# Weight dequantisation moved out of the projection stage onto GpSimd in the attention stage, its loads issued twice a slot by SyncE

## What is computed

```
x = x + attention(layernorm(x))      # 32 heads of width 16, causal, biases on q, k, v, o
x = x + ffn(layernorm(x))            # gate/up 512x1792, down 1792x512, 4-bit weights held as int32
x = x + topk_mlp(layernorm(x))       # 1376 wide, the half with the smallest |silu| set to zero
x = x + ffn(layernorm(x))            # the same quantised weights again
```

## Time and profile before

| what | us |
|---|---|
| median of 3 runs (2161.17, 2175.11, 5822.98) | 2175.11 |
| the profiled execution, its own time | 2164.9 |
| its span, first to last instruction | 2163.1 |
| stage 1 (start to the last matmul) | 184.4 |
| stage 2 (187.7 to the end of slot 15) | about 583 |
| mean granted TensorE clock | 0.969 |

### The profile page before, as it was taken

The page is one execution under the profiler, slowest core; times in us unless marked ns, Lnnn a source line. Parts: engine busy times, 40 slices in busy tenths (PEclk is TensorE's granted clock), DMA queues, the critical chain, the costliest instruction groups (busy, mean ns, idle before and its releaser), DMA issues. The chain is left out here.

```text
span 2163.1 us, 38405 instructions
## 1 busy us (share of the span) xinstructions
PE 2014.5 (93%) x14288; PEld 1236.3 (57%) x14288; DVE 1565.1 (72%) x2736; ACT 1020.2 (47%) x1658; POOL 560.5 (26%) x587
## 2 busy tenths in 40 slices
PE   5887999999999977899999999999999999999989
PEld 2342344444444344677667667666666666666756
DVE  6775677777777432169888988978889889788941
ACT  3221356565655621156366454553664545535511
POOL 2223453842523332111210311212103112121221
PEclk9997799999999988999999999999999999999999
DMA  7766235432333164020222013013130130131000
GB/s 258 234 214 176 70 95 137 126 86 68 93 95 83 33 196 167 9 98 1 87 72 100 6 53 120 6 53 119 59 125 1 54 115 1 53 115 53 11 11 11
DMA packets 115656, 187.35 MB, mean 87 GB/s; under 512 B 43200, under 2 KB 68176, under 8 KB 115520
## 3 DMA queue, kind: packets, MB, share of 16 engines
q1 hardware_dynamic: 91344, 133.22, 19.9%
q0 software_dynamic: 9088, 32.12, 5.3%
q10 hardware_dynamic: 15088, 20.19, 2.7%
HBM read 151.59 MB, written 33.62 MB: 86 GB/s over the span
## 5 line engine op out<-in xcount | busy, mean ns | idle before, releaser
L842 DVE TENSOR_REDUCE mx<-s 128x1 f32<-128x512 f32 (+3 forms) x608 | 380.9, 660 | 128.8 <-PE s L731 75.0
L823 ACT ACTIVATE pr<-s 128x1024 f32<-128x1024 f32 (+3 forms) x352 | 300.7, 868 | 243.8 <-PE s L750 181.7
L1467 ACT ACTIVATE kept<-ax,T 128x1376 f16<-128x1376 f32 x248 | 357.0, 1439 | 122.0 <-DVE T L1541 116.1
L1535 DVE TENSOR_SCALAR_CACHE_REDUCE junk<-ax,T 128x1376 f16<-128x1376 f32 x248 | 406.5, 1639 | 3.1 <-DVE T L1528 0.5
L1326 POOL TENSOR_TENSOR lohi<-h,lohi 128x256 f16<-128x256 f32 x224 | 173.6, 775 | 872.9 <-ACT lohi L1478 872.7
L1364 PE MATMUL ga<-xT_f,w_gate 128*128 128x256 f16 x2688 | 332.7, 274 | 7.9 <-DVE h L1592 4.9
L1374 PE MATMUL acc<-w_down,lohi 128*128 128x512 f16 x1344 | 326.3, 379 | 8.7 <-POOL lohi L1326 8.7
L1364 PE MATMUL ub<-xT_f,w_up 128*128 128x256 f16 x2688 | 331.6, 273 | 0.0
L1364 PEld LDWEIGHTS ga<-xT_f,w_gate 128*128 128x128 f16 x2688 | 263.3, 98 | 79.9 <-DVE h L1592 7.5
L1364 PEld LDWEIGHTS ub<-xT_f,w_up 128*128 128x128 f16 x2688 | 263.9, 98 | 31.2
L728 PE MATMUL s<-K,Q 65*128 65x512 f16 (+3 forms) x768 | 245.2, 345 | 26.3 <-DMA K<-onerow 13.5
(11 more groups left out here) (142 smaller groups left out, 2352.5 us busy)
## 6 DMA issues: line engine op xcount, KB each, us to landing
ring<-wgu_scr SPq DMA_DIRECT2D x64, 688.0 KB, 5.3
ring<-wd_scr SPq DMA_DIRECT2D x24, 768.0 KB, 4.7
wgu_scr<-tk_h POOLq DMA_DIRECT2D x16, 344.0 KB, 6.0
q_scr<-qk_h ACTq DMA_DIRECT2D x16, 256.0 KB, 4.0
k_scr<-qk_h ACTq DMA_DIRECT2D x16, 256.0 KB, 2.5
v_scr<-v_f ACTq DMA_DIRECT2D x16, 256.0 KB, 2.9
Q<-q_scr SPq DMA_DIRECT2D x32, 128.0 KB
K<-k_scr SPq DMA_DIRECT2D x32, 128.0 KB
```

The lines of the kernel that those rows point to most:

```text
L823: nc.scalar.activation(pr[:, kb % 2, j0:j1, 0:w], scores, ACT.Exp, scale=SCALE).then_inc(e2_ok, 1)
L842: nc.vector.tensor_reduce(dst, s1[u % 2][:, 0:(j1 - j0) * w].rearrange("p (j k) -> p j k", k=w), AX.X, ALU.max).then_inc(r1_ok, 1)
L1467: nc.scalar.activation(kept[0][:, :], ax[k % 2][:, 1, :], ACT.Sign, scale=-1.0, bias=TF[:, 1:2], accum_out=cnt[:, 1:2]).then_inc(c1_ok, 1)
L1535: nc.vector.tensor_scalar(junk[:, :], ax[k % 2][:, 0, :], TF[:, 0:1], -float(KZERO), ALU.is_lt, ALU.add, accum_out=cnt[:, 0:1]).then_inc(c ...
```

## The change

`phase_project` loses the 16 pieces on all five engines. With them gone it is rewritten in these points: ACT writes `qk_f` and the float16 `qk_h` from PSUM, two activations in a row, and DVE's cast is gone; the stores move from ACT to SP and have four buffers instead of two; the transposes have four PSUM banks instead of two; the raw weights have three buffers instead of two; the q weights are loaded and split in four parts, the first two tiles are normalised before the others, and k and v weights are split in slots 0 and 1.

`phase_attend` gets all quantised weights: 32 pieces 128x448 of gate and up and 14 pieces 128x512 of down, each five POOL operations. The third block's weights come in 32 pieces 128x344 and 11 of 512 columns, each with three POOL operations and one store instead of two. POOL's work is spread over 32 half slots. SP issues all loads, in two packs a slot, one between half 0 of Q and K and the maxima row, one between V and the output's store; each load waits for the buffer of three (or four) pieces before. V beside ones of slot n + 1 is done at the middle of slot n in POOL's program. SP's loop is written out.

```diff
             for s in range(SLOTS):
                 c, u = s // SPC, s % SPC
                 if u < QK_SLOTS:
...
-                    nc.scalar.activation(qk_f[:, u % 2, :], pmm[u % 4][:, :], ACT.Identity,
-                                         bias=bias_qk[:, u // KB, u % KB:u % KB + 1], scale=QS / (XS * WS)
-                                         ).then_inc(qkf_ok, 1)
+                    nc.scalar.activation(qk_f[:, u % 2, :], pmm[u % 4][:, :], ACT.Identity, bias=bias,
+                                         scale=QS / (XS * WS))
+                    wait(act, qk_st[u % NST], 16 * (v // NST))
+                    nc.scalar.activation(qk_h[:, u % NST, 0, :], pmm[u % 4][:, :], ACT.Identity, bias=bias,
+                                         scale=QS / (XS * WS)).then_inc(qkf_ok, 1)
+                if s < 2:
+                    weight_hi(s + 1)
...
-                    nc.vector.tensor_copy(qk_h[:, u % 2, 0, :], qk_f[:, u % 2, :]).then_inc(qkh_ok, 1)
-                    dve.wait_ge(qkh_ok, v + 1)
...
+        NDQ = len(dq_pieces)
+        UNITS = 2 * NQ
+        dq_unit = [m * UNITS // NDQ for m in range(NDQ)]
+        dq_load = [dq_unit[m - NDB] + 1 if m >= NDB else 0 for m in range(NDQ)]
...
+        tk_unit = [m * UNITS // NTK for m in range(NTK)]
+        tk_load = [tk_unit[m - NRAW] + 1 if m >= NRAW else 0 for m in range(NTK)]
...
+            def load_pieces(unit):
+                for m in range(NDQ):
+                    if dq_load[m] == unit:
+                        width, wsrc, zsrc, ssrc, _dst = dq_pieces[m]
+                        wait(sp, dq_lo, m - NDB + 1)
+                        for dst, src in ((dq_w, wsrc), (dq_z, zsrc), (dq_s, ssrc)):
+                            sp.dma_start(dst[:, m % NDB, 0:width], src).then_inc(dq_in[m % NDB], 16)
...
+            for n in range(NQ):
+                if n + 2 < NQ:
+                    load_qk(n + 2, 0)
+                load_pieces(2 * n + 1)
+                if n + 1 < NQ:
+                    maxima_row(n + 1)
+                if n + 2 < NQ:
+                    load_qk(n + 2, 1)
+                    load_v(n + 2)
+                load_pieces(2 * n + 2)
+                store(n)
...
+            def dequantise(m):
+                width, _w, _z, _s, (hi, lo) = dq_pieces[m]
+                value, raw, zero, scale = (t[:, m % NDB, 0:width] for t in (dq_f, dq_w, dq_z, dq_s))
+                pool.wait_ge(dq_in[m % NDB], 48 * (m // NDB + 1))
+                nc.gpsimd.tensor_tensor(raw, raw, zero, ALU.subtract).then_inc(dq_sub, 1)
+                pool.wait_ge(dq_sub, m + 1)
+                nc.gpsimd.tensor_scalar(value, raw, WS, 1.0, ALU.mult, ALU.mult).then_inc(dq_up, 1)
+                pool.wait_ge(dq_up, m + 1)
+                nc.gpsimd.tensor_tensor(value, value, scale, ALU.mult).then_inc(dq_mul, 1)
+                pool.wait_ge(dq_mul, m + 1)
+                nc.gpsimd.tensor_copy(hi, value).then_inc(dq_hi, 1)
+                pool.wait_ge(dq_hi, m + 1)
+                nc.gpsimd.tensor_tensor(lo, value, hi, ALU.subtract).then_inc(dq_lo, 1)
+
+            beside_ones(0)
+            for unit in range(UNITS):
+                if unit % 2 and unit // 2 + 1 < NQ:
+                    beside_ones(unit // 2 + 1)
+                for m in range(NDQ):
+                    if dq_unit[m] == unit:
+                        dequantise(m)
+                for m in range(NTK):
+                    if tk_unit[m] == unit:
+                        split_weights(m)
```

More of the change, by code:

```diff
@@ L116, in phase_project @@
     QK_SLOTS = 2 * KB
+    NTR = 4
+    NST = 4
     with ExitStack() as ctx:
@@ L184, in phase_project @@
-        NPIECE = len(pieces)
+        qk_st = [sem(f"qk_st{i}") for i in range(NST)]
+        v_st = [sem(f"v_st{i}") for i in range(NST)]
         SLOTS = NCH * SPC
-        slot_of = [2 + n * (SLOTS - 5) // NPIECE for n in range(NPIECE)]
-        piece_at = {s: n for n, s in enumerate(slot_of)}
-        assert len(piece_at) == NPIECE and slot_of[-1] + 2 < SLOTS
         RSTD_AT, XN_AT = 2, 4
         block = ctx.enter_context(nc.Block())
[L194 to L198, removed]
@@ L200, in _, with load_x @@
         @block.sync
         def _(sp):
[L202 to L208, removed]
+            def load_x(c):
+                wait(sp, xn_ok, TPC * (c - 1))
+                sp.dma_start(xin[:, c % 2, :, :], x[c * CW:(c + 1) * CW, :].rearrange("(t p) d -> p t d", p=P)
+                             ).then_inc(x_in[c % 2], 16)
@@ new lines, in _ @@
+            for s in range(SLOTS):
+                c, u = s // SPC, s % SPC
+                if u < QK_SLOTS:
+                    n = QK_SLOTS * c + u
+                    sp.wait_ge(qkl_ok, n + 1)
+                    sp.dma_start((q_scr, k_scr)[u // KB][(u % KB) * P:(u % KB + 1) * P, :, c * CW:(c + 1) * CW],
+                                 qk_h[:, u % NST, :, :]).then_inc(qk_st[u % NST], 16)
+                else:
+                    n = TPC * c + u - QK_SLOTS
+                    sp.wait_ge(vf_ok, n + 1)
+                    sp.dma_start(v_scr[n * P:(n + 1) * P, :], v_f[:, n % NST, :]).then_inc(v_st[n % NST], 16)
+                if s == 3:
+                    load_x(2)
+                if s == SPC + 2:
+                    load_x(3)
@@ L224, in _ @@
+            for i in range(NST):
+                sp.wait_ge(qk_st[i], 16 * QK_SLOTS // NST * NCH)
+                sp.wait_ge(v_st[i], 16 * TPC // NST * NCH)
         @block.gpsimd
@@ L529, in phase_attend @@
         o_out = [sem(f"o_out{i}") for i in range(2)]
-        tk_in = [sem(f"tk_in{i}") for i in range(2)]
+        tk_in = [sem(f"tk_in{i}") for i in range(NRAW)]
         tk_up = sem("tk_up")
@@ new lines, in load_pieces @@
+            def load_pieces(unit):
[6 more added lines that the diff above has]
+                for m in range(NTK):
+                    if tk_load[m] == unit:
+                        rows, width, src, _dst = tk_pieces[m]
+                        wait(sp, tk_lo, m - NRAW + 1)
+                        sp.dma_start(tk_raw[0:rows, m % NRAW, 0:width], src).then_inc(tk_in[m % NRAW], 16)
@@ new lines, in _ @@
+            for n in range(2):
+                for f in range(2):
+                    load_qk(n, f)
+                load_v(n)
+            load_pieces(0)
+            maxima_row(0)
+            for n in range(NQ):
[9 more added lines that the diff above has]
+                store(n)
```

363 lines of the change are left out of this document (134 added, 229 removed).

## The result

| | us |
|---|---|
| before, median on the chip of this comparison | 2171.14 |
| after, median | 2156.12 |
| ratio, with 95% interval | 0.9947 (0.9929 to 0.9965) |
| profiled execution of after, span | 2154.3 (before 2163.1) |

The time lies in the forecast's range and the sign is right, but of 24 us forecast 11 to 15 came. Behind that stand two errors of opposite sign, which partly cancel: stage 1 gained 36.0 us, not 30, and stage 2 lost 26, not 6.

The account below looks back on a forecast made before the run. PE bounds stage 2; in stage 1 PE waits for `xn` from DVE. Stage 1 was to lose 30 us (32.5 - 5.5 + 3.4) and stage 2 to add 6: 2164.9 - 30 + 6 = 2141 us, range 2126 to 2176.

Parts of the forecast that it names:

- Term 1: Stage 1: PE's waits for `xn` and the slow restarts after them go, 32.5 us less.
- Term 2: Stage 1: new short waits of PE's transposes for `xn`, 0.4 us for each of 12 groups, 5.5 us more in all.
- Term 3: Start of stage 1: PE's first product comes 3.4 us earlier, at 14.9 us.
- Term 4: Stage 2: POOL's added work fits, 25 us of a 33.3 us slot, price 0.
- Term 5: Stage 2: the maxima row queues behind the pack's loads, 0 to 1.3 us late in 8 slots, 5 us more.
- Term 6: Stage 2: DVE's small maximum ahead of the row is slowed by a running POOL operation; price 0, bound 7 us.
- Term 7: Stage 2: POOL's stores of split weights, 43 instead of 38, collide once more with a row, 1 us more.
- The slower rival: Stage 2: maxima row late in every slot behind transfers issued ahead, 42 us over 15 slots; 2177, up to 2189 us; 12%.
- Its second price: Stage 2, row late in every slot: 15 slots cost 54 us if the pack moves at 246 GB/s instead of 280.

Follow-up runs that it names:

- experiment 4: The changed kernel, but SP issues both packs of weight loads behind V, none ahead of the maxima row: 2130.28 us, ratio 0.9813.
- experiment 7: The changed kernel with POOL's scalings written with one operation, without the second multiplication by 1: ratio 0.995.
- experiment 2: The changed kernel, but SP waits for the maxima row to land before issuing half 1 of Q and K: 2147 us, ratio 0.9899.
- experiment 6: Kernels with both packs behind V, plus chosen amounts of data ahead of the maxima row in five slots: 2145.9, 2142.3, 2149.0 and 2138.6 us.
- the first experiment: The changed kernel with SP's odd pack of loads issued behind the maxima row instead of ahead of it: 2319 us, ratio 1.0594.
- The first two dose kernels: Both packs behind V, chosen data ahead of the row in five slots: 2145.9 us; the same with SP waiting there for the row before half 1: 2142.3.
- the one with the splits ahead: The changed kernel with the k and v weights split ahead of slot 0 instead of in slots 0 and 1: 2160.7 us, one run.

## Why the forecast was half right

- **Term 1** (waits and slow restarts, 32.5): right in kind. Without the start, stage 1 gained 32.3 us. Removing the pieces alone gave 26.9, and the other 5.4 is about what banks, buffers and cast are worth.
- **Term 2** (new short waits, 5.5) is the term of stage 1 that was mis-sized: one wait of 0.92 us was seen. I had added up a chain of 3.5 us behind each slot and compared it with 3.0; with two buffers one wait is 2.72 us, with four 0.92.
- **Term 3** (start, 3.4): 3.7.
- **Term 4** (POOL, price 0): right, with 18 to 29 us a slot, 22 in the mean, instead of 25, and shown by experiments 4 and 7. The two-operation form costs less than half, not the same.
- **Term 5** (the row behind the pack, 5 us) is where the forecast failed. The mechanism is the forecast's, and so is the group of slots, those with two quantised pieces ahead; the size was five times too small. Four things were wrong in it. The landing: the sum had the pack landed 7.8 to 8.4 us after its first issue. In slots 3, 8 and 9 it was (7.9 to 8.3), in the four late slots it took 11.2 to 11.7. Half 1 of Q and K, issued right behind the row and left out of the sum, is 1.2 to 2.2 us of that (experiment 2); the rest stays open. The sum itself: 0.6 us of lateness was multiplied by 8 slots as if it were the cost, though the prediction's own rows priced a late row at 1.5 to 2.8 us, which would have given 12 to 22. The price: it was taken from waits of about 1 us, the only ones the trace had; waits of 3.6 to 4.2 us cost 5.6 to 9.5 with the clock. And the prediction's statement that a wait under two us costs no clock is not so: one of 1.41 us cost 5.8 (slot 10 of experiment 6), and its own first row, 0.97 us in a slot of 36.0 at clock 0.95, already spoke against it. Of the eight slots with two pieces ahead four were late by 3.6 us or more (0, 1, 2 and 10) and slot 11 by 1.1; in slots 3, 8 and 9 PE waited 0.24 us or less.
- **Term 6** (port), price 0: the price was right, but after is no test of the mechanism. There the small maximum took 0.17 to 0.18 us in 14 of 16 slots because POOL, waiting for the pack, ran nothing beside it. In the kernel of experiment 4 POOL does, and the maximum then lasts until POOL's operation is over:

```profile
362.82 1.04 POOL L650 TENSOR_TENSOR w_gate<-dq_w,w_gate 128x448 f16<-128x448 f32 x1
...
363.04 0.85 DVE L801 TENSOR_TENSOR mx<-mx 128x16 f32<-128x16 f32 x1
```

  Such waits of up to 0.68 us lengthened that kernel's slots by 0.4 us at most. This agrees with the rule of the Trainium skill, page "SBUF — State Buffer", section "SBUF: two separate sides", that the second of the two waits out the whole instruction of the first. The row that the prediction set against it, beside a scaling of one operation, stays an exception.
- **Term 7** (stores, 1 us): no run takes it apart.
- The slower rival had the same mechanism in every slot, at 2.8 us. It was right in that a late row can cost more than forecast (up to 9.5 us) and wrong in where. Its second price has no ground: term 5 implies about 200 GB/s (1.55 MB in 7.8 us), not 280. In the first experiment, where a wait stands in almost every slot, its time came and was exceeded: 2319.

## What to carry to other kernels

A background load is placed by what will be needed next, not by what it stands in front of now: here the slot had one place with 20 us of slack, and moving the pack by one consumer was worse than leaving it. A short transfer on the critical path is delayed by what is issued behind it and on other queues as well, so bulk has to be separated from it in time. A wait of PE must be priced with the clock, and as a range: over all slots of these kernels waits of 0.8 to 1.3 us cost 1.0 to 3.0 us, and waits of 1.4 to 7.2 us between 1.1 and 5.4 times themselves. The length of the wait alone does not give the price.

## What the runs showed of the hardware

- POOL's multiplication of 448 columns takes 564 ns with two scalar operations and 1329 ns with one, on the same data; of 344 columns 477 and 1070.
- The first attention slot takes 38.1 to 38.8 us in most executions, 44.4 in one and 50.3 to 51.1 in five, with the same work: the clock, at half when the slot begins, comes back some 16, 29 or 43 us into it. The first two dose kernels have the same program up to slot 4, and one took 38.7, the other 50.7. The two kernels whose slots are shown are after and the one with the splits ahead:

```profile
191.01:229.26 38.25, 36.11 (x237) 15.24 (x238) 24.42 (x40) 18.32 (x21) 8.69 (x11) 0.81 0.18 44
```

```profile
190.50:241.60 51.10, 49.32 (x238) 19.13 (x239) 25.59 (x41) 18.52 (x21) 10.13 (x13) 0.57 0.18 49
```

  That is 12 us of chance in one profile, as much as the change is worth, so the slots are compared from the second on. What decides it stays open.
- The pack of slot 10 made PE wait 1.4 to 3.4 us in three executions of nearly the same program, and 2.7 to 6.1 in the six with the order of after. What sets it within that is open too.
